# First attention's probabilities: one unit in four multiplied and clipped on GpSimd instead of VectorE

## What is computed

```python
x = x + _L0_xattn_ref(_layernorm(x), ctx, ctx, Wq, bq, ...)   # 16 heads of 16
x = x + _L0_ffn_ref(_layernorm(x), w_gate, w_up, w_down)      # FP4-quantized weights and inputs
x = x + _L1_xattn_ref(_layernorm(x), ctx, ctx, mask, ...)     # 16 heads of 64, masked
x = x + _L1_ffn_ref(_layernorm(x), w1, b1, w2, b2)            # fixed point, piecewise GELU
```

```python
scores = jnp.einsum('bhqd,bhkd->bhqk', Qh, Kh) / scale
scores = scores - jnp.max(scores, axis=-1, keepdims=True)
attn = jax.nn.softmax(jnp.clip(scores, -CLAMP, CLAMP), axis=-1)
attn = jnp.clip(attn, EPS, None)                 # EPS = 1e-12
attn = attn / jnp.sum(attn, axis=-1, keepdims=True)
ctx = jnp.einsum('bhqk,bhkd->bhqd', attn, Vh)
```

## Time and profile before

| | |
|---|---|
| median of 3 runs | 927.66 us (927.36 to 927.87) |
| the profiled execution's own time | 927.82 us |
| its span in the trace | 926.0 us |
| TensorE busy | 900.5 us (97%) |
| VectorE busy | 669.8 us (72%) |
| ScalarE busy | 602.1 us (65%) |
| GpSimd busy | 204.6 us (22%) |
| granted TensorE clock | full, save for the last stage |
| opening, 20 to 98 us: TensorE, VectorE, ScalarE busy | 70.5, 72.7, 62.1 of 78 us |
| one crossing, 264 to 323 us: the same | 58.5, 50.2, 48.4 of 59 us |

### The profile page before, as it was taken

One profiled execution on the slowest core, in us unless ns is written; L12 is line 12 of the kernel. 1 busy time (PEld: TensorE's weight loads), 2 busy tenths in 40 slices (PEclk: granted clock), 3 DMA queues, 4 the chain that ended last, 5 costly groups with the idle time before them and its releaser, 6 DMA issues.

```text
span 926.0 us, 16209 instructions
## 1 busy us (share of the span) xinstructions
PE 900.5 (97%) x5610; PEld 601.8 (65%) x5610; DVE 669.8 (72%) x2179; ACT 602.1 (65%) x1671; POOL 204.6 (22%) x316
## 2 busy tenths in 40 slices
PE   6899999999999999999999999999999999999998
PEld 3555576767665567576675566667757655757786
DVE  5999883763989786475598978367478988837568
ACT  3888425972789643795378953499257984269845
POOL 3211001862000000486000000077400000028600
PEclk9999999999999999999999999999999999999999
DMA  9500000000000000000000010000000000000000
GB/s 294 212 1 2 29 1 23 2 1 1 1 1 25 1 28 24 1 1 2 1 0 8 18 29 1 24 1 1 1 0 1 19 7 1 1 0 2 2 1 23
DMA packets 14560, 18.35 MB, mean 20 GB/s; under 512 B 3088, under 2 KB 11664, under 8 KB 14480
## 3 DMA queue, kind: packets, MB, share of 16 engines
q1 hardware_dynamic: 12288, 15.40, 5.0%
q10 hardware_dynamic: 2064, 1.91, 0.7%
q0 software_dynamic: 128, 0.01, 0.0%
HBM read 15.21 MB, written 2.10 MB: 19 GB/s over the span
## 4 chain that ended last, share of the span: by engine, by line
PE 76%; DVE 13%; ACT 8%; issue 3%; DMA 1%; SPq 0%; DVEq 0%; ACTq 0%
PE bank L1243 28%; PE bank L1258 10%; PE bank L1526 6%; PE bank L1624 6%; PE bank L1506 6%; PE bank L1358 5%; PE bank L1414 4%; ACT ring L671 4%; DVE row_max L1050 3%; PE bank L1391 3%; PE bank L1481 1%; PE bank L1492 1%; PE bank L1251 1%; PE bank L1430 1%; ACT ring L715 1%
## 5 line engine op out<-in xcount | busy, mean ns | idle before, releaser
L463 POOL TENSOR_TENSOR rstd<-var_eps,minus_half 128x2 f32<-128x2 f32 x32 | 23.3, 734 | 533.1 <-DVE var_eps L886 533.1
L481 POOL TENSOR_TENSOR ring<-ring,row_inv 128x256 f32<-128x256 f32 x192 | 112.1, 613 | 95.4 <-DVE row_inv L1145 95.4
L556 ACT ACTIVATE ring<-bank 128x512 f32<-128x512 f32 x224 | 123.6, 612 | 14.1 <-PE bank L1258 12.6
L1258 PE MATMUL bank<-ident_s,ring 128*128 128x128 f32 x768 | 105.0, 279 | 5.1 <-DVE ring L1058 2.7
L1258 PEld LDWEIGHTS bank<-ident_s,ring 128*128 128x128 f32 x768 | 82.8, 141 | 39.2 <-issue 15.7
L715 ACT ACTIVATE ring<-ring,row_max 128x256 f32<-128x256 f32 x192 | 95.1, 497 | 17.3 <-DVE row_max L1138 17.3
L671 ACT ACTIVATE ring<-bank,row_max 128x256 f32<-128x256 f32 x192 | 88.4, 496 | 5.7 <-DVE row_max L1050 5.7
L1138 DVE CUSTOM_DVE_ANT_0 ring<-bank,maskbias 128x256 f32<-128x256 f32 x192 | 70.7, 420 | 23.4 <-issue 23.4
L1050 DVE TENSOR_REDUCE row_max<-bank 128x2 f32<-128x512 f32 x128 | 79.4, 684 | 5.9 <-PE bank L1391 5.2
L1243 PE MATMUL bank<-wgu_s,act_s 128*128 128x352 f32 x256 | 78.4, 459 | 0.0
L1243 PE MATMUL bank<-ctxT_s,wk_s 128*128 128x512 f32 x160 | 76.4, 600 | 0.0
(11 more groups left out here) (192 smaller groups left out, 1753.3 us busy)
## 6 DMA issues: line engine op xcount, KB each, us to landing
x_s<-x SPq DMA_DIRECT2D x4, 512.0 KB, 3.9
ctxT_s<-ctxT SPq DMA_DIRECT2D x4, 512.0 KB, 4.2
w_s<-w SPq DMA_DIRECT2D x2, 1024.0 KB, 16.3
out<-act_s SPq DMA_DIRECT2D x16, 128.0 KB, 1.7
wk_s<-wk SPq DMA_DIRECT2D x1, 1024.0 KB, 13.4
wv_s<-wv SPq DMA_DIRECT2D x1, 1024.0 KB, 14.7
wq_s<-wq SPq DMA_DIRECT2D x1, 1024.0 KB, 16.2
wo_s<-wo SPq DMA_DIRECT2D x1, 1024.0 KB, 17.5
```

What stands on the lines that cost most here:

```text
L481: ins = pool.tensor_tensor(probs1[i % PRING1][:, a, :], probs1[i % PRING1][:, a, :], row_inv[:, i, a:a + 1].to_broadcast([P, SEQ]), ALU.mult)
L556: act.activation(probsT[u % TRING][:, :, :].rearrange("p a q -> p (a q)"), psum(at, key)[:], ACT.Copy).then_inc(drain(at, key), 1)
L1258: ins = pe.transpose(psum(at, key)[:, c * SEQ + a * P:c * SEQ + (a + 1) * P], tile[:, a, c * P:(c + 1) * P], ident_s[:])
```

## The change

A constant POOL_UNIT = 2 names the third unit of every round. VectorE still inverts its sums, then leaves it; GpSimd waits for the inverse and does the same two instructions (tensor_scalar, multiply by a column and take the maximum with 1e-12, 128 x 256 each) in place. TensorE waits for a second semaphore, clipped0_pool, before this unit's transposes; the counts of both come from normalized0. In the opening GpSimd's list takes these in turn with the weight pieces, and the mask's bias stands behind round 1's unit, without its wait for nine maxima. In each crossing eight such units stand behind the last ln_power.

```diff
+def normalized0(u):
+    return u // 4 + 1 if u % 4 == POOL_UNIT else u + 1 - (u + 3 - POOL_UNIT) // 4
...
+            def normalize0(g, u):
+                pool.wait_ge(inv0, g * UNITS + u + 1)
+                for a in range(2):
+                    ins = pool.tensor_scalar(probs0[u % PRING0][:, a, :], probs0[u % PRING0][:, a, :], row_inv[:, u, a:a + 1], CLIP,
+                                             ALU.mult, ALU.max)
+                ins.then_inc(clipped0_pool, 1)
...
-            for n in POOL_PIECES:
-                if n == 2:
+            for r in range(ROUNDS0):
+                normalize0(0, 4 * r + POOL_UNIT)
+                if r % 2 == 0:
+                    multiply_piece(POOL_PIECES[r // 2])
+                if r == 1:
                     pool.wait_ge(mask_loaded, 16)
-                    pool.wait_ge(max0, 9)
                     mask_to_bias()
-                multiply_piece(n)
...
+                for r in range(ROUNDS0):
+                    normalize0(g + 1, 4 * r + POOL_UNIT)
...
+                    if u % 4 == POOL_UNIT:
+                        return
                     dve.wait_ge(inv0, units + u + 1)
...
-                    pe.wait_ge(clipped0, group * UNITS + u + 1)
+                    if u % 4 == POOL_UNIT:
+                        pe.wait_ge(clipped0_pool, group * ROUNDS0 + normalized0(u))
+                    else:
+                        pe.wait_ge(clipped0, group * (UNITS - ROUNDS0) + normalized0(u))
```

More of the change, by code:

```diff
@@ L49 @@
 AHEAD, BEHIND = 1, 1
+POOL_UNIT = 2
 FIRST_SCORES_AFTER = 4
@@ L348, in xattn_ffn_twice @@
         scaled, steps_ready, rounded = sem("scaled"), sem("steps_ready"), sem("rounded")
-        max0, inv0, clipped0 = sem("max0"), sem("inv0"), sem("clipped0")
+        max0, inv0, clipped0, clipped0_pool = sem("max0"), sem("inv0"), sem("clipped0"), sem("clipped0_pool")
         bias_ready, exp1, inv1, norm1 = (sem(n) for n in ("bias_ready", "exp1", "inv1", "norm1"))
```

## The result

The changed kernel takes 935.37 us (median of 4, 935.0 to 935.88), the kernel before 927.76 beside it (927.36 to 927.91): ratio 1.0083, interval 1.0071 to 1.0095, 7.6 us longer. The profiled execution's span is 933.7 us against 926.0.

What follows compares the result with a forecast made beforehand. TensorE was taken to fill the crossings, with the chain passing through ScalarE's exponentials and VectorE's fourth units. From 927.82 us, +0.6 for the crossings and +0.5 for the opening gave 928.9; range 926.0 to 935.5.

Steps and rivals of the forecast that it cites:

- GpSimd's price: GpSimd's multiplication of the third unit: 1.18 us a pair, from a two-input row of 612 ns; bounds 0.4 and 0.83 an instruction.
- Whether TensorE waits: Third unit's transposes in the crossings: GpSimd ready after 1.42 of 2.16 us, no wait; waiting would begin at a 1.92 us pair.
- rival 3: GpSimd's instruction takes 0.83 us, making VectorE 0.56 us late at crossing and opening passages: +5.7, 933.5 us; chance 25%.
- Collisions in the crossings: Fourth unit's multiplication on VectorE starts 0.10 us late beside GpSimd's pair, twice per crossing on the chain: +0.6 us.
- The opening: Rounds 1, 2, 4 and 7: moved mask block +0.8, old block gone -0.83, small delays from GpSimd's pair; sum +0.5 us.
- The relief: Third unit's multiplication off VectorE: worth nothing in the crossings, at most 0.73 us in the opening's round 2.
- (a): Sign on GpSimd's new line: near 0.6 us an instruction and 1.2 us a pair.
- (b): Sign on VectorE's fourth-unit multiplications: slightly longer than the others; near 0.35, 0.9 or 1.18 us would favour rival explanations.
- (c): Sign on TensorE: its transposes wait for GpSimd nowhere.
- (d): Sign in the opening on VectorE: long instruction at 42.86 gone, one of 1 to 1.8 us between 37 and 40 us.
- (e): Sign on a crossing's chain: distance between the two fourth units, 13.69 us before, longer by 0.1.
- 4: Every collision of VectorE and GpSimd costs a fixed 0.82 us, in crossings and opening: +8.5, 936.3 us; chance 12%.

Runs made afterwards that it cites:

- the best version: Kernel before, with the mask's bias made first, x's bias later, and the first half of each fourth unit multiplied on GpSimd: 925.66 us, ratio 0.998.
- the kernel with the relief alone: Changed kernel with the third unit's multiplication left out altogether, GpSimd doing nothing in its place and TensorE waiting for the inverse: 927.72 us, ratio 1.0001.
- the kernel with half of the unit: Changed kernel with only the third unit's first 128 queries on GpSimd and the others on VectorE: 928.36 us, ratio 1.0005.
- the kernel with the mask out of VectorE's way: Kernel before, with GpSimd making the mask's bias first and x's bias behind round 4's row maxima: 926.79 us, ratio 0.9991.
- the kernel without the wait for GpSimd: Changed kernel with GpSimd's pair on a scratch tile, the third unit unmultiplied and TensorE waiting for the inverse alone: 930.69 us, ratio 1.0033.
- the third unit's kernel at the low price: Changed kernel with GpSimd's pair as a two-input tensor_tensor, inverse broadcast, clip left out on the third unit: 929.97 us, ratio 1.0033.

## Why the prediction was right or wrong

**What bounds the kernel**: right. The busy shares said nothing of the cost, the crossing's chain through VectorE was the loop to beat, and the crossings had next to nothing to give (0.1 and 0.2 us in the best version).

**GpSimd's price**: wrong, and this is the step on which the number fell. The prediction took 1.18 us for the pair, by "the row nearest in form", and 0.83 us an instruction as the upper bound, from the converting row. It was 2.28, 1.14 an instruction, and by the prediction's own last sign ("I am wrong if GpSimd's op is far from 0.6 us") that settles it. Neither of the two arguments carried: that an instruction reading one tensor needs less than one reading two is refuted by 849 against 613 ns, and the converting L474 is cheaper for each element (2.77 us for 1024, 2.7 ns each) than this form (1.14 us for 256, 4.5 ns each), so it was no upper bound. The trace of before held no float32 tensor_scalar of this size on GpSimd, and the range should have been left open upwards for that.

**Whether TensorE waits**: the rule was right (from a pair of 1.92 us on; the loop gives 2.0, and one of 1.9 to 2.0 was waited for off the chain and cost nothing by it), the answer was wrong because of the price. Worse, rival 3, the long instruction, was priced through VectorE's delay alone, and ended at a pair of 1.64 us, short of that threshold. The wait is the larger term, 4.7 of the 7.6 us.

**Collisions in the crossings**: right in kind and, at the price assumed, in size (0.10 a passage, the distance 13.79 for 13.69). At the true price the rule that VectorE is let in 0.2 us ahead of the pair's end would have made 0.24 + 2.28 - 0.2 - 1.12 = 1.2 us; it was 0.28. VectorE gets in between GpSimd's two instructions and beside the second (last section). The collisions were over-priced for long instructions and the wait wasn't priced at all; the two errors partly made up for each other. The range held by this, by 0.13 us, and by luck: its upper end, 935.5, lies 2.0 us above rival 3's 933.5, the highest sum it was to cover, and no term of the prediction gives those 2.0 us.

**The opening**: +0.5 forecast, +1.3 measured, some +1.5 at the price assumed. The mask's move by itself was sized rightly as far as can be told (0.8 less 0.83; 927.41 against 927.56, with an interval of some 0.8 us to either side). Behind a pair on GpSimd it hit two of VectorE's instructions: 0.97 and 0.54 us with the short pair; with the long pair and the mask it was 0.29 and 0.60, and 0.40 more on the fourth pair of round 2.

**The relief**: at most 0.73 us forecast, all of it in round 2. That round gave none, since ScalarE's exponentials are what VectorE waits for next; the 0.37 us by which the rounding came earlier were there before the round began, and by the end nothing was left of them. By the marker the kernel with the relief alone is ahead by 0.7 at the opening's end, of which 0.3 is the mask's move (96.5 for 96.8 in the kernel that has only that), and by 0.1 at the last crossing; where the rest goes in the later groups stays open.

**Signs named ahead**: (a) failed, 1.14 for 0.6; (b) the fourth unit's two instructions take 0.44 and 0.55 us beside 0.35 (0.56 is the longest anywhere): nearer the forecast than the 0.9 of rival 3, though GpSimd's instruction was longer than that rival's; (c) failed, 23 waits of the weight load; (d) the instruction at 42.86 is gone, and the blocks between 37 and 40 us were two of 0.3 and 0.6 and not one of 1 to 1.8; (e) the distance no longer runs through VectorE in the changed kernel; with GpSimd's price at 612 ns it came out as forecast. Of the rivals, 3 has the right direction and the right cause, with another main mechanism; 4 came nearest in time (936.3) for a wrong reason, since no collision costs a fixed 0.82 us.

The Trainium skill, "SBUF — State Buffer", section "Who interferes with whom", says that a VectorE instruction in a 2-port mode, which tensor_scalar can enter, and a GpSimd instruction block each other, the second comer for the whole of the other's instruction. This case's runs don't bear that out for these instructions: VectorE's multiplication beside GpSimd's 1.14 us took 0.55 for 0.35 us. In which mode it ran no trace shows.

## What to carry to other kernels

Before work is moved to an idle engine, write down the loop that its result closes, here exponentials, inverse, multiplication, transposes, copies, next exponentials, and compare the whole with the kernel's longest loop: the new engine's latency counts in it, not its throughput. Where the trace has no row of the very form (operation, number of operations, constant or column), don't bound its price by a row of another form; leave the range open, and price every branch through each threshold that the sum itself has named. If an engine is slower at a step, give it a part small enough to be done beside the rest of the same step, and keep its long instructions away from the other engine's chain.

## What the runs showed of the hardware

- On GpSimd a float32 tensor_scalar of 128 x 256 took 849 ns with one operation and a constant, 976 with a column, 1068 with two operations and constants, 1142 to 1167 with a column and a clip; the tensor_tensor of the same size took 612 to 613 (all medians; the kernel with one operation in place of two had 950 and 1004 for the column alone).
- VectorE's in-place multiplication beside it. In the changed kernel GpSimd's two instructions ran from 36.53 and from 37.65 us; VectorE's first ran from 37.38 for 0.44 us (0.35 alone), the second for 0.55, wholly within GpSimd's second, which itself was late by 0.03 us at most; the two second ones in the timeline:

```profile
37.74 0.55 DVE L1077 TENSOR_SCALAR big_k<-big_k,row_inv 128x256 f32<-128x256 f32 x1
...
37.65 1.17 POOL L495 TENSOR_SCALAR big_k<-big_k,row_inv 128x256 f32<-128x256 f32 x1
```

- Beside the mask's instruction of 2.77 us VectorE was late by up to 0.97 us, and sometimes not at all. In the kernel with the relief alone the fourth pair of round 1 lies wholly within it and takes its usual 0.62 us; in the kernel with half of the unit L851 at 38.93, within it too, takes its usual 0.19, where its twin in the changed kernel takes 0.79. The relief kernel's rows:

```profile
37.04 0.62 DVE L1073 TENSOR_SCALAR big_k<-big_k,row_inv 128x256 f32<-128x256 f32 x2
...
36.18 2.77 POOL L481 TENSOR_SCALAR maskbias<-mask_s 128x1024 f32<-128x1024 uint8 x1 [4.04 <-DVE row_inv L1068]
```

- So overlap by itself doesn't tell who is late, or by how much. What rule covers all of these is open.
- It goes the other way too: where VectorE starts first, GpSimd's is late. 1.29 to 2.09 us in place of 1.14 in the best version. The small instruction at 21.29 us shows it by the order alone. In four of the fourteen profiles it starts 0.16 to 0.28 us behind VectorE's two-input L840 (or its twin) and takes 0.78 to 0.90 us, to just behind that one's end; in the other ten it starts ahead and takes 0.24 or 0.25, as in the kernel with the mask out of VectorE's way:

```profile
21.30 0.24 POOL L492 TENSOR_SCALAR b_s<-b_s 128x8 f32<-128x8 f32 x1 [11.33 <-DMA wo_s<-wo]
```

- TensorE's granted clock fell in the opening of two profiled executions behind a stretch in which TensorE stood idle. Windows of 1 us of the kernel without the wait for GpSimd, with TensorE's busy time and its granted clock behind the brackets (1.00 is 2.4 GHz, 0.50 is 1.2):

```profile
43.00:44.00 1.00, 0.00 (x0) 1.00 0.00 0
...
47.00:48.00 1.00, 1.00 (x10) 0.50 0.00 0
```

Over 43 to 44 us TensorE did nothing, over the next two it was busy for 0.57 and 0.82 us; from 46 to 50 it had half its clock or not much more (0.62, 0.50, 0.50, 0.67). The idle stretch doesn't decide it: the kernel before did nothing over 43 to 44 us either, was busy for 0.65 and 0.93 over the next two, and kept its full clock:

```profile
47.00:48.00 1.00, 1.00 (x12) 1.00 0.00 0
```

The changed kernel's profile shows a clock of 1.00 throughout the opening. In the third unit's kernel at the low price it also fell behind the opening, where TensorE was busy throughout. In the window below the mean clock is 0.95, which costs 0.05 x 32 = 1.6 us, nearly all of the 1.8 us between its executions (before: 1.00 in the same stretch). That kernel's window:

```profile
98.00:130.00 32.00, 32.00 (x123) 0.95 0.07 21
```
